# A routed decoder layer on one core: each tile's second expert layer runs two steps after its first instead of three

## The reference

```
t = x.reshape(b * f, d)                        # 2048 tokens of 256
logits = silu(t @ rw1 + rb1) @ rw2 + rb2       # 8 experts
vals, idx = top_k(logits, 2)
w = softmax(the two chosen logits)
eh = silu(t @ ew1[e] + eb1[e])                 # 256 -> 512
eo = eh @ ew2[e] + eb2[e]                      # 512 -> 256
y = t + sum over the two experts of w * eo
```

## Time and profile before

| what | value |
|---|---|
| median of three runs | 514.31 us (511.88 to 514.64) |
| the profiled execution, its own time | 516.64 us |
| its span | 514.8 us |
| PE busy over the span | 474.3 us (92%) |
| DVE, ACT, POOL busy | 351.5 us (68%), 279.1 us (54%), 172.5 us (33%) |
| mean granted TensorE clock | 0.982 |
| mixture stage, from the first layer of tile 0 to the second layer of tile 38 | 349.8 to 501.0 us |

### The profile page before, as it was taken

How to read it: one execution, slowest core, us unless ns; L and a number is a source line. 1 busy time by engine, 2 the same in 40 slices (tenths; PEclk the granted TensorE clock), 3 DMA queues, 4 the chain that set the end, 5 groups by cost and what they waited for, 6 DMA issues and landing times.

```text
span 514.8 us, 11626 instructions
## 1 busy us (share of the span) xinstructions
PE 474.3 (92%) x3734; PEld 337.6 (66%) x3734; DVE 351.5 (68%) x837; ACT 279.1 (54%) x715; POOL 172.5 (33%) x184
## 2 busy tenths in 40 slices
PE   6999989999999999999999999898988989888980
PEld 2456479765569956559965567787866767666760
DVE  5744776796866786867688787986666745444567
ACT  4263666346556526547526665636656557656650
POOL 1230233040124040214221202343458455556441
PEclk9899999999999999999999999998999999999995
DMA  8901000315210035230032335081132282122566
GB/s 330 351 0 43 0 2 1 120 45 206 81 42 0 11 111 178 74 117 0 1 122 78 126 125 228 22 335 45 44 117 74 64 282 72 51 78 66 154 200 228
DMA packets 20411, 54.39 MB, mean 106 GB/s; under 512 B 3365, under 2 KB 9774, under 8 KB 19600
## 3 DMA queue, kind: packets, MB, share of 16 engines
q1 hardware_dynamic: 16336, 43.32, 23.8%
q0 software_dynamic: 3744, 9.47, 6.4%
q10 hardware_dynamic: 288, 1.05, 0.6%
HBM read 36.98 MB, written 17.76 MB: 106 GB/s over the span
## 4 chain that ended last, share of the span: by engine, by line
PE 53%; issue 20%; DVE 16%; POOL 5%; ACT 1%; DMA 1%; DVEq 1%; another core or an unknown queue 1%; POOLq 0%; ACTq 0%; SPq 0%
PE pj L1461 14%; PE op L1696 7%; PE pj L1675 4%; PE pj L1780 4%; PE tpA L1790 3%; PE tpB L1790 2%; PE sc L1780 2%; PE sc L1652 2%; PE op L1780 2%; POOL pn L459 2%; DVE up_f L1227 1%; POOL rstd L429 1%; PE sc L1548 1%; DVE stats L767 1%; PE tpA L1792 1%
## 5 line engine op out<-in xcount | busy, mean ns | idle before, releaser
L1461 PE MATMUL pj<-up,up_f 128*128 128x512 f16 x480 | 108.6, 381 | 3.6 <-DVE down L1305 1.1
L1461 PEld LDWEIGHTS pj<-up,up_f 128*128 128x128 f16 x480 | 46.0, 98 | 59.5 <-DVE rope L937 5.3
L677 ACT ACTIVATE p<-sc,nm 128x128 f32<-128x128 f32 x128 | 45.4, 369 | 39.2 <-DVE nm L1300 39.0
L459 POOL TENSOR_TENSOR pn<-p,inv 128x256 f32<-128x256 f32 x64 | 37.9, 614 | 80.4 <-DVE inv L1259 80.4
L477 POOL DMA_INDIRECT cst<-rows,src_row x39 | 46.0, 1179 | 39.6 <-DVE wch L1250 17.9
L488 POOL DMA_INDIRECT picked<-wch,dst_row x39 | 40.7, 1043 | 29.9 <-DVE wch L1250 13.7
L429 POOL TENSOR_TENSOR rstd<-veps,nhalf 128x4 f32<-128x4 f32 (+1 forms) x13 | 12.7, 976 | 103.5 <-DVE veps L775 103.2
L549 ACT ACTIVATE down<-pj,bias 128x512 f32<-128x512 f32 x48 | 32.5, 685 | 26.4 <-PE pj L1461 26.3
L1461 PE MATMUL pj<-up_f,up 128*128 128x512 f16 x192 | 43.4, 379 | 0.0
L518 ACT ACTIVATE up_f<-sc 128x512 f16<-128x512 f16 x39 | 23.1, 592 | 36.4 <-remote 29.4
L1696 PE MATMUL op<-wch,outs 128*128 128x256 f16 x240 | 40.2, 273 | 0.0
(11 more groups left out here) (267 smaller groups left out, 1062.5 us busy)
## 6 DMA issues: line engine op xcount, KB each, us to landing
raws<-in_staged SPq DMA_DIRECT2D x12, 512.0 KB, 5.3
split<-halved SPq DMA_DIRECT2D x12, 512.0 KB, 4.0
down<-split SPq DMA_DIRECT2D x4, 1024.0 KB
rows<-row SPq DMA_DIRECT2D x4, 528.0 KB
small<-in_x SPq DMA_DIRECT2D x4, 512.0 KB, 3.5
up<-in_ctx SPq DMA_DIRECT2D x4, 512.0 KB, 4.8
v<-in_w SPq DMA_DIRECT2D x2, 1024.0 KB, 9.2
resid<-outs SPq DMA_DIRECT2D x4, 512.0 KB
```

The source lines that it names most:

```text
L459: pool.tensor_tensor(pn2[:, n % 2, k], p2[:, n % 2, k], inv2[:, n % 2, k].unsqueeze(2).to_broadcast([P, 2, P]), ALU.mult)\
L677: last = act.activation(p2[:, s, i, :], sc[s][:, i * P:(i + 1) * P], ACT.Exp, bias=nm2[:, s, i:i + 1], scale=1.0, accum_out=sum2[:, s, i:i ...
L1461: last = pe.matmul(out, w(c), v(c), start=(i == 0), stop=(i == len(terms) - 1))
```

## The change

LAG goes from 3 to 2, so PE runs the second layer of tile t - 2 in step t, right behind the first layer of tile t, and DVE weighs tile t - 3 in step t. TRAIL, which was 2 * LAG + 2 = 8, is written as 8 and stays. In DVE's step hidden_low(t - 2) goes from behind weigh_out and take to the head of the step. Since the second layer of tile 0 now comes before last_hidden(1) on PE, which had held the waits for the two banks tpA and tpB, these waits are added ahead of it.

```
 SLOTS = 3
 STEPS = 6
-LAG = 3
+LAG = 2
 TILES = (B * L * 2 + E * (P - 1)) // P
-TRAIL = 2 * LAG + 2
+TRAIL = 8
...
             for t in range(TILES + LAG + 1):
+                if 2 <= t < TILES + 2:
+                    hidden_low(t - 2)
                 if t >= LAG + 1:
                     weigh_out(t - LAG - 1)
                 if t + 2 < TILES:
                     take(t + 2)
                 if t == 0:
                     rows_low_half(1)
-                if 2 <= t < TILES + 2:
-                    hidden_low(t - 2)
...
                 if t < TILES:
                     first_layer(t, own[k])
                 if t == LAG:
+                    pe.wait_ge(tpA_free, TPA * G + 2)
+                    pe.wait_ge(tpB_free, TPB * G + 2)
                     pe.wait_ge(split_in, 64)
                     pe.wait_ge(b2_lo_in, 16)
```

## The result

| kernel | median | lowest to highest | runs |
|---|---|---|---|
| before | 514.31 us | 511.88 to 516.17 | 9 |
| after | 518.46 us | 516.68 to 521.33 | 9 |

The ratio is 1.0082 (95% interval 1.006 to 1.0105): the change makes the kernel slower by 0.8%, some 4 us. Run once more beside the last experiments, it took 517.96 us (11 runs) against 514.87 (28 runs), a ratio of 1.0059 (1.0037 to 1.0082). So the loss is 0.6 to 0.8%, and both intervals leave out 1.

A forecast was written before the change was run, and what follows sets the result against it. PE, busy for 92% of the span, was taken as the bound, its even part held by a loop of unnamed cause. Even part 0, opening with steps 4 to 11 +1.7, end -0.5: +1.2 us, 514.3 to 515.5; range 509.5 to 520.

The forecast's parts named there:

- rival (b): Steps 2 to 11: tile 12's drag and DVE's hold on PE both stay, +2.7 to +5 us, 517 to 519.5; chance 0.13.
- drag: Tile 12's first layer in the kernel before takes 4.4 us instead of 1.4; 3.0 us that might stay or go.
- First, the even part: Middle of the stage: low halves come 0.6 to 0.85 us before PE needs them; taken as 0 us.
- the beat: Even part: PE has a hole every second tile, so two tiles take some 7.5 us where their matmuls take 6.1.
- a wait for L1227 after 420: Even part: PE waiting there for DVE's line L1227 was named as showing the forecast wrong, by (c).
- (c): Even part gets bound by h_lo, 0.5 us in 13 pairs of tiles, 6.5 us slower, 522 us; chance 0.10.
- (a): Even part: the beat changes and PE's holes go in three pairs or more, 500 to 512 us; chance 0.20.
- Second, the opening: Opening steps: PE waits for low halves, last_hidden(1) and logits come late; PE 4.1 us behind, counted within the third part.
- Third, steps 4 to 11: Low halves hold second layers, the 4.1 us are made up; +0.2 without the drag, +3.2 with it, middle +1.7 taken.
- a sign of being wrong: Steps up to 12: tile 12's first layer whole in 1.5 us and the time still rising would show the forecast wrong.
- Fourth, the end: After the last first layer: three second layers remain instead of four, a 0.43 us wait won; -0.5 us, bounds -0.6 and +0.1.
- rival (d): Opening: the clock falls in the new waits, 1.7 us of PE's work lost, +2.9 us, 517.2; chance 0.07.

The follow-up runs named there:

- e1: The change with the low half back in its old place on DVE, behind weighing and take; 547.34 us, ratio to before 1.0648.
- e6: The kernel before with one more PE wait in each second layer, on the bank's last weighing; 517.46 us, ratio to before 1.0008.
- e5: The change with the turn and the last round's piece ahead of the second layer on PE in steps 2 and 3; 514.26 us, ratio to before 0.9989.
- e10: The change with tile 1's low half ahead of last_hidden(1) on DVE; 515.76 us, ratio to before 1.0019.
- e11: e5 with TRAIL 7 instead of 8, each scatter one step sooner behind its gather; 515.81 us, ratio to before 1.002.
- e3: The change from step 13 on only, lag of three before that, with a written-out bank wait; 519.18 us, ratio to before 1.0074.
- e7: e3 without the written-out bank wait, low half at the head one step later; 518.74 us, ratio to before 1.0044.
- e8: e7 with the switch to a lag of two in step 20 instead of 13; 519.18 us, ratio to before 1.0045.
- e4: The change through step 12 only, lag of three from step 14, with a written-out bank wait; 520.22 us, ratio to before 1.0095.
- e12: The kernel before with TRAIL 7 instead of 8, nothing else changed; 520.29 us, ratio to before 1.0096.

## Why the prediction was right or wrong

The time (518.46, and 517.96 in the second measurement) lies within the range of 509.5 to 520, but above the forecast of 515.5 and its +0.5 to +2.5 us. The loss lies in the interval of rival (b), +2.7 to +5, but that rival's drag isn't there. The range held it because it had been drawn wide for the rivals, so that it holds the time is luck.

**First, the even part: the beat right, its sum not nothing.** From 400 to 450 one second layer waits for a low half, 0.56 us, and the beat stays. By the prediction's own sign a wait for L1227 after 420 would speak for (c), but 0.56 us once is far from 0.5 us in 13 pairs. That the low half at the head is what saves it is shown by e1 (+6.5%). Rivals (a) and (c) are out: the 7.5 us for two tiles become 7.2, which wins some 2.6 us (below) where I had taken 0, but the holes stay, while (a) had them go.

**Second, the opening: right in every number here.** Predicted and measured: second layer of tile 0 359.75 and 359.63, DVE's last_hidden(1) 363.65 and 363.64, second layer of tile 1 366.1 and 366.17, logits 367.8 and 367.80, choose 369.85 and 369.68, second layer of tile 2 372.5 and 372.54. That the two bank waits at t == LAG cost nothing follows from the same row: PE's wait before 359.63 ends with the low half. e6 tried another bank wait, and that one was free.

**Third, steps 4 to 11: the size as taken, for another reason.** Second layers of tiles 3 to 9 were forecast for 375.8, 379.0, 383.6, 387.2, 391.1, 394.3 and 397.4, and started at 376.0, 379.1, 383.7, 387.2, 390.9, 395.2 and 398.6. The prediction had a low half hold each of them; the rows show such a wait for tiles 7 and 8 alone. Tile 12's first layer was done at 403.0 instead of 401.3: +1.7 us, the middle that was taken. But the middle stood for a drag that stays by half, and the drag is gone altogether: tile 12's first layer, 24 matmuls from 401.07, has no hole. By the prediction's own sum that left +0.2. The other 1.5 us came before it. Up to tile 7 forecast and trace agree to 0.2 us; then the low half of tile 8 takes 1.87 us instead of 0.68, beside POOL's operation from 392.99, and tiles 8 and 9 start 0.9 and 1.2 us late. The prediction didn't have this. The same low half takes 1.86 to 1.87 us in the second trace of the change, in e5 and in e10, each time started 0.21 us behind POOL's operation. In e1 another low half falls on its last 0.4 us and takes 0.96. In all five it ends 0.54 to 0.55 us after POOL's operation, as if it had waited for that. In e11 and in the kernel before, no low half falls on it, and none is slow. So the size was met by luck. And what came, tile 12's first layer whole and the time still up, is what the prediction had named as a sign of being wrong.

**Fourth, the end: it won almost nothing, and a step before it was missing.** Since after runs its second layers a step sooner, I compare by work done: the time at which first layers up to tile f and second layers up to tile s are both through. Before it is the start of tile s's second layer and 1.4 us, after the start of tile s + 1's.

| f and s done | before | after | after is later by |
|---|---|---|---|
| 12 and 9 | 401.3 (tile 9's layer starts late, at 399.7, and takes 1.6) | 403.0 | 1.7 |
| 13 and 10 | 402.8 + 1.4 = 404.2 | 406.1 | 1.9 |
| 34 and 31 | 481.23 + 1.4 = 482.63 | 481.94 | -0.7 |
| 35 and 32 | 485.36 + 1.4 = 486.76 | 486.92 | 0.2 |
| 36 and 33 | 488.43 + 1.4 = 489.83 | 490.46 | 0.6 |
| start of the last second layer | 499.47 | 500.04 | 0.6 |

So the even part gives back 2.6 us, more than the 1.9 that the opening and steps 4 to 11 had cost. The step of five DMAs and the one behind it take 1.3, and the end gains under 0.1 where -0.5 was forecast. What was to be won there, PE's wait of 0.43 us, has only moved: the last tile's second layer now waits 0.44 us for its low half, and the prediction had it follow without a gap. It didn't have the 1.3 us either: I had counted POOL's operations, which are the same, but not how many of them are ready in a row. In hundredths, +1.93 - 2.62 + 1.32 - 0.06 = +0.57, and the span is 0.6 us longer. The sum for the profiled execution was 517.8; it took 517.22, and 517.98 the second time. It came near because terms of both signs were missing.

**The step that failed is the last one, from the trace to the median:** "That execution lies 2.3 us above the median of the runs, so the median goes from 514.3 to 515.5." It took for granted that whatever made that execution 2.3 us longer than its median would be there in after's profiled execution too. After's profiled executions lie 1.2 us below and at their medians. The loss of 4.15 us, where +1.2 was forecast, is therefore not in the pair of traces, which has +0.6. The part of 4 us that no pair of traces shows had to come from the medians of the experiments, and these say:

- 1.0082 and 1.0059 with the change, 0.9989 with the same lag and PE's pieces in the other order in steps 2 and 3, 1.0019 with one low half moved on DVE. So the order of the opening costs 0.4 to 0.9%, most of the loss. That is shown. That it is the whole loss is not: e11 has e5's order too and comes to 1.002 (1.0006 to 1.0034).
- The rest, lag of two from step 13 or 20 on, costs 0.4 to 0.7% when it is done alone (e3, e7, e8), the opening alone 0.95% (e4), with the clock's fall in its trace. The halves don't add up to the change, since each has a switch in it; the second half's own price isn't settled. In the traces e5 has done the work up to tile 12's first layer 1.3 us ahead of before (400.0 against 401.3) and starts the last second layer 2.1 us ahead, so there the second half wins; its median is 0.6 us ahead, with 1 in the interval. These don't give a price.
- Which executions of before are the quick ones (511.9 to 514), and what they leave out, no trace shows. Their times go with the granted clock: of the 28 runs of before beside the last group, the ten at 0.984 or more took 514.25 us in the mean, the four under 0.98 took 515.5. Why the medians lie 4.15 us apart and the traces 0.6 stays open.

**The clock, rival (d).** In the stretch with the new waits of 0.94, 2.10 and 1.54 us the granted clock was 1.00, the level of 2.4 GHz, in both traces of the change. In e4, with the same waits, it was 1.00 there too, but fell in a stretch behind it:

```profile
384.00:388.50 4.50, 4.09 (x26) 2.79 (x27) 3.92 (x13) 0.76 (x2) 1.16 (x1) 0.62 0.21 65
```

The fall on which the rival was built, 0.53 from 349.8 to 353.4, stands ahead of the opening and isn't tied to the wait before it. All 14 kept traces have this wait, 2.11 or 2.12 us for ACT's copy near 348; in the 3.6 us that begin 1.25 us after it, the granted clock is 1.00 in eight of them, both traces of the change among these, and 0.53 to 0.69 in six (before, e5, e6, e7, e8, e10). Nor did the fall cost before its 1.7 us: PE's turn behind it starts at 356.26, after a wait of 0.39 us for the gather, and in the change, without the fall, at 356.04, after 1.23 us for the same gather; the change had been 0.2 us ahead since 346. And the nine runs of the change had a granted clock of 0.986 in the mean, no less than the runs of before, of which 17 are on record with the first group (0.983). As a cause of these 4 us the clock is out. The Trainium skill, "TensorE: Matmul & The Clock Gate", section "HAM oscillation — how this bites in real kernels", tells of a kernel in which each short group of work begins cold after a wait; its waits are longer than those here, and the opening of the change, three groups behind waits at full clock, pays no such price.

**The beat.** In the rows of the change, e5 and e11 PE's holes near 480 end with POOL's run of indirect DMAs; where the run is one shorter, they end sooner. The drag of tile 12 is there when POOL runs without a pause (before, e11) and gone when it pauses (the change, e5). Why, no row says: PE's holes carry "issue", and the waits of the others "remote". A kernel with the scatters on another engine wasn't tried, so that POOL's run is the cause is only argued.

## What to carry to other kernels

A shorter lag between two stages turns the work that used to have a step of slack into a wait, and what stands behind that wait in the same queue is late with it: look first for one-time pieces there (here a router's chain) and put them ahead of the waiting instruction. If a stage is pulled forward, the helper that feeds it has to move to the head of its queue in the same edit; without this the change would have cost 6.5%. And when a profiled execution lies off the median of its kernel, a sum made on its trace doesn't forecast the next median (here +1.2 forecast, +0.6 between the traces, +4.15 between the medians): keep that distance as an uncertainty of both signs, rather than carry it over.

## What the runs showed of the hardware

- Two executions of the same program agree in the start of each second layer to 0.16 us over the first 90 us of the stage, and part only later (tile 31 at 477.6 and 478.4, tile 32 at 481.9 and 481.8, tile 34 at 490.5 and 491.7).
- In e3 a weighing waited 6.23 us for a scatter of 128 rows to land, beside the residual's load of 2 MB, issued at 417.45 (POOL began the scatter at 418.59, and the weighing started at 427.80); in the change two weighings wait for scatters at that place (425 to 429), 2.22 and 1.66 us.
- One step of TRAIL is worth 1% in a kernel with a lag of three (e12, 1.0096): a scatter that waits stands at the head of POOL's queue, in front of a gather that could go.
- DVE's low half of 128x512 elements, 0.68 us by itself, took 1.86 to 1.87 us in four traces where it started 0.21 us behind a POOL operation over 128x704 elements (1.53 us), and 0.96 in e1, where it met only the end of one. It ended 0.54 to 0.55 us after POOL's operation in all five. Two weighings that fell on that operation in the kernel before kept their 0.48 us.
- After the same wait of 2.1 us, ahead of the same work, the granted clock was 1.00 in eight traces and 0.53 to 0.69 in six.
